# Main stage of a graph layer: a pair's 1/sqrt(variance) from its bits and three Newton steps on VectorE, in place of ScalarE's Ln and Exp and one step

## What is computed

```python
def _layernorm(x, axis=-1, eps=1e-05):
    m = jnp.mean(x, axis=axis, keepdims=True)
    v = jnp.var(x, axis=axis, keepdims=True)
    return (x - m) / jnp.sqrt(v + eps)

# _L0_gnn_ref(feat, dist, W, w_att_src, w_att_dst, src, dst):
ft = (feat @ W).reshape(n, H, OUT)                    # 4 heads of 64
e = e_src[src] + e_dst[dst];  e = where(e >= 0, e, 0.2 * e)
ex = exp(e - emax[dst]);  denom = segment_sum(ex, dst)
out = segment_sum(ft[src] * (ex / denom[dst] * dist), dst)
# _L0_ffn_ref: router (256 -> 128 -> 6), top 2 of 6 experts, three layers of 256 each
x = x + _L0_gnn_ref(_layernorm(x), ...)
x = x + _L0_ffn_ref(_layernorm(x)[None], ...)[0]
```

## Time and profile before

| | us |
|---|---|
| median of three runs | 3443.87 |
| the profiled execution's own time | 3440.41 |
| its span | 3438.6 |
| preparation and features | 0 to about 350 |
| main stage | about 350 to 2623 |
| expert stage | 2623 to 3438.6 |
| busy: PE, DVE, ACT, POOL | 2431.9, 2002.0, 1558.5, 2092.5 |
| L982 gathers, 1568 | 1504.5 |
| L1039 messages, 294 | 672.3 |
| table loads ahead of Ln and Exp, 63 each | 80.8 each |

### The profile page before, as it was taken

How to read it: one execution, slowest core, us unless ns; L and a number is a source line. 1 busy time by engine, 2 the same in 40 slices (tenths; PEclk the granted TensorE clock), 3 DMA queues, 4 the chain that set the end, 5 groups by cost and what they waited for, 6 DMA issues and landing times. The chain is left out here.

```text
span 3438.6 us, 59846 instructions
## 1 busy us (share of the span) xinstructions
PE 2431.9 (71%) x15542; PEld 1943.8 (57%) x15543; DVE 2002.0 (58%) x4402; ACT 1558.5 (45%) x3023; POOL 2092.5 (61%) x2064
## 2 busy tenths in 40 slices
PE   0177466666777777777777777777664999999995
PEld 0155355555555565556555555555553787777774
DVE  0354444555667677777777777777776733333332
ACT  0066223343445455555555555555552554444442
POOL 0000677777777777767666665556530677777775
PEclk9999678778788788878878888887776999999997
DMA  0366455555555555655555554445435044445443
GB/s 27 103 197 214 146 161 159 157 169 164 168 166 179 164 179 173 179 163 168 153 159 151 155 156 142 147 131 152 135 92 86 24 78 79 81 78 81 79 80 48
DMA packets 244778, 457.70 MB, mean 133 GB/s; under 512 B 56010, under 2 KB 161818, under 8 KB 243805
## 3 DMA queue, kind: packets, MB, share of 16 engines
q0 software_dynamic: 114816, 262.31, 31.8%
q1 hardware_dynamic: 89644, 155.19, 14.1%
q10 hardware_dynamic: 40226, 39.16, 3.3%
HBM read 376.24 MB, written 81.66 MB: 133 GB/s over the span
## 5 line engine op out<-in xcount | busy, mean ns | idle before, releaser
L982 POOL DMA_INDIRECT m_rows<-table,src_col x1568 | 1504.5, 960 | 922.8 <-issue 698.0
L1307 PE MATMUL m_A<-m_msg,m_by_edge 128*128 128x260 f32 x3920 | 1240.7, 482 | 297.8 <-DVE m_msg L1039 231.7
L1307 PEld LDWEIGHTS m_A<-m_msg,m_by_edge 128*128 128x128 f32 x3920 | 933.6, 245 | 514.6 <-DVE m_msg L1039 270.9
L1039 DVE TENSOR_TENSOR m_msg<-m_rows,m_A 128x2048 f32<-128x2048 f32 x294 | 672.3, 2287 | 41.5
L1170 ACT ACTIVATE m_apart<-m_drow,nid 128x1024 bf16 x296 | 340.0, 1148 | 420.8 <-SPq L953 420.8
L1294 PE MATMUL m_E<-m_look_parts,m_by_node 128*128 x7080 | 254.3, 167 | 272.2 <-DVE m_by_edge L1009 198.4
L1294 PEld LDWEIGHTS m_E<-m_look_parts,m_by_node 128*128 128x128 bf16 x7080 | 234.5, 97 | 372.0 <-issue 341.3
L1009 DVE TENSOR_TENSOR m_by_edge<-row,m_E 128x512 f32<-128x512 f32 x590 | 401.9, 681 | 5.3 <-ACT m_E L1167 3.2
L1508 POOL DMA_INDIRECT out<-x_con,x_to_i x206 | 329.2, 1598 | 103.4 <-issue 78.8
L1173 ACT ACTIVATE m_by_node<-m_apart,m_one 128x1024 bf16<-128x1024 bf16 x296 | 339.9, 1148 | 9.7
L1178 ACT ACTIVATE m_z<-m_z 128x32 f32<-128x32 f32 x294 | 67.1, 228 | 578.4 <-DVE m_z L1033 482.8
(11 more groups left out here) (243 smaller groups left out, 2357.7 us busy)
## 6 DMA issues: line engine op xcount, KB each, us to landing
m_drow<-edges SPq DMA_DIRECT2D x196, 512.0 KB
m_rows<-table,src_col POOLq DMA_INDIRECT x1568
ydram<-m_y ACTq DMA_DIRECT2D x49, 264.0 KB
m_xb<-xpad ACTq DMA_DIRECT2D x50, 256.0 KB
table<-f_rowbuf SPq DMA_DIRECT2D x14, 910.0 KB, 4.6
xpad<-f_xin SPq DMA_DIRECT2D x14, 896.0 KB, 7.1
out<-m_x ACTq DMA_DIRECT2D x48, 256.0 KB
f_xin<-in_x SPq DMA_DIRECT2D x13, 896.0 KB, 6.0
```

The lines of the kernel that those rows point to most:

```text
L982: nc.gpsimd.indirect_dma_start(rows[:, g % RING, j, :], None, table, bass.IndirectOffsetOnAxis(ap=K.src_col[:, g, j:j + 1], axis=0)).then_ ...
L1039: v.tensor_tensor(msg[q][:, :, 0:D].rearrange("p j (h n) -> p j h n", h=HEADS), rws[:, :, 0:D].rearrange("p j (h n) -> p j h n", h=HEADS), ...
L1307: m = t.matmul(psA[i % 2][:, 0:ROW], by_edge[i % 3][:, j, :], msg[i % 2][:, j, :], start=(j == tiles[0]), stop=(j == tiles[-1]))
```

## The change

ScalarE's `guess` goes from the main stage, with its three semaphores. VectorE computes the first guess of the reciprocal root itself from the bits of the variance (a shift right by one at the end of `take_sums`, a subtraction from the constant 0x5f3759df at the start of `normalize`, both on int32), and does three Newton steps in place of one. The constant `RSQRT_BITS` was in the file already. Nothing else is moved.

```diff
--- before.py
+++ after.py
@@ -904,6 +904,7 @@
         y = sb("y", [P, 2, YW])
         den, stats, mv = sb("den", [P, 2, HEADS]), sb("stats", [P, 2, 6]), sb("mv", [P, 2, 2])
         var, inv, newton = [sb(n, [P, 2]) for n in ("var", "inv", "newton")]
+        half_bits = sb("half_bits", [P, 2], I32)
         yT = sb("yT", [P, 2, 2 * P])
         rhT = sb("rhT", [P, 2 * P])
         plan = sb("plan", [1, PLAN], I32)
@@ -926,7 +927,6 @@
         summed, added = sem("summed"), sem("added")
         drel_made, z_added, z_sloped = sem("drel_made"), sem("z_added"), sem("z_sloped")
         z_kept, wd_made, slot_free = sem("z_kept"), sem("wd_made"), sem("slot_free")
-        asked, given, between = sem("asked"), sem("given"), sem("between")
         plan_in, look_steps = sem("plan_in"), sem("look_steps")
         light_steps, apart_made, node_onehots = sem("light_steps"), sem("apart_made"), sem("node_onehots")
         weights_in, ready = sem("weights_in"), sem("ready")
@@ -1047,7 +1047,7 @@
                 to = flat(sums[:, bass.ds(before % AR, 1), :])
                 v.tensor_tensor(to, to, psA[1 - q][:, 0:ROW], ALU.add).then_inc(added, 1)
 
-            A_STEPS, L_STEPS = 11, 16
+            A_STEPS, L_STEPS = 13, 25
 
             def take_sums(pair, adds):
 
@@ -1076,18 +1076,23 @@
                 for i in range(2):
                     st.did(v.bn_aggr(mv[:, i, :], stats[:, i, :]))
                 st.settle()
-                v.tensor_scalar(var[:, :], mv[:, :, 1], EPS, None, ALU.add).then_inc(asked, 1)
+                st.did(v.tensor_scalar(var[:, :], mv[:, :, 1], EPS, None, ALU.add))
+                st.settle()
+                st.did(v.tensor_scalar(half_bits[:, :], var[:, :].bitcast(I32), 1, None, ALU.arith_shift_right))
                 assert st.n == A_STEPS, st.n
 
             def normalize(pair):
 
                 st = Steps(dve, light_steps, pair * L_STEPS + A_STEPS)
-                dve.wait_ge(given, pair + 1)
-                st.did(v.tensor_tensor(newton[:, :], inv[:, :], inv[:, :], ALU.mult))
-                st.settle()
-                st.did(v.scalar_tensor_tensor(newton[:, :], newton[:, :], -0.5, var[:, :], ALU.mult, ALU.mult))
-                st.settle()
-                st.did(v.scalar_tensor_tensor(inv[:, :], newton[:, :], 1.5, inv[:, :], ALU.add, ALU.mult))
+                st.settle()
+                st.did(v.tensor_scalar(inv[:, :].bitcast(I32), half_bits[:, :], -1.0, RSQRT_BITS, ALU.mult, ALU.add))
+                for _ in range(3):
+                    st.settle()
+                    st.did(v.tensor_tensor(newton[:, :], inv[:, :], inv[:, :], ALU.mult))
+                    st.settle()
+                    st.did(v.scalar_tensor_tensor(newton[:, :], newton[:, :], -0.5, var[:, :], ALU.mult, ALU.mult))
+                    st.settle()
+                    st.did(v.scalar_tensor_tensor(inv[:, :], newton[:, :], 1.5, inv[:, :], ALU.add, ALU.mult))
                 dve.wait_ge(y_stored, 16 * (pair + 1))
                 dve.wait_ge(y_turned, pair + 1)
                 st.settle()
@@ -1207,9 +1212,6 @@
                 relu_router(pair)
                 keep_logits(pair)
 
-            def guess(pair):
-                rsqrt_guess(nc, 2, var, inv, asked, given, between, pair + 1)
-
             count = lambda r: act.snap(r, min_val=0, max_val=NPAIR)
             index = lambda r: act.snap(r, min_val=0, max_val=NPAIR - 1)
 
@@ -1236,8 +1238,6 @@
                         with act.If(count(routed) < count(done)):
                             copy_turned(index(routed))
                     if i % HI == 1:
-                        with act.If(count(done) < count(ready_pairs)):
-                            guess(index(done))
                         with act.If(count(routed) < count(done)):
                             relu_router(index(routed))
                     if i % HI == 2:
@@ -1255,7 +1255,6 @@
                         with act.If(count(routed) < pair):
                             route(index(routed))
                         act.reg_mov(routed, pair)
-                        guess(act.snap(pair, min_val=0, max_val=NPAIR - 1))
                         store_light(act.snap(pair, min_val=0, max_val=NPAIR - 1))
                     act.reg_mov(done, due)
             now = count(done)
```

## The result

| | before | after |
|---|---|---|
| median of the runs, us | 3444.98 (3442.36 to 3450.21) | 3610.64 (3603.95 to 3613.23) |
| ratio to before, 95% interval | | 1.0476 [1.0457, 1.0495] |
| the profiled execution | 3440.41 | 3610.73 |

The change makes the kernel 166 us slower. The forecast was 3418 us, 27 us faster.

A forecast was written before the change was run, and what follows sets the result against it. Gathers were taken to bound the main stage until 1460 us, VectorE after. 35 pairs at 0.64 us (22.4) plus 4.1 for the last pair, 26.5 us, took 3443.9 to 3417.4, written as 3418; range 3405 to 3431.

The forecast's parts named there:

- Bounds of the stages: Main stage: GpSimd's gathers set the time up to 1460 us, VectorE behind it, where its microseconds count.
- The wait that goes: VectorE's L1086 waiting for ScalarE's guess behind 1460 us: 85.6 us, 35 times, 2.45 us each, would be removed.
- The links: Eight added small VectorE instructions per pair, each waiting for the last: 0.20 us for two, 0.195 for six, 1.57 us.
- a sign of being wrong: Among the signs against the forecast: an integer step on VectorE taking over 0.25 us.
- a gather held back by the step: Rival: new tensor_scalars lengthen GpSimd's gathers by 0.2 us each in 13 gather-bound pairs, 5 us, giving 3423; 6%.
- The entrance: VectorE's branch into normalize after L1048: 0.24 us idle, 0.5 at most; gain 0.64 us a pair.
- The last pair: Main stage's end, no items left: 1.77 us instead of 5.87 to the last old step, gain 4.1 us.
- Slower: Rival: VectorE's longer loop body costs code supply, 1.0 us per turn in 26 turns cancelling the gain, 1.5 giving 3456; 5%.
- given back: Rival: TensorE sets the pace after pairs, L1048 waits instead, half of 22.4 us goes, giving 3429; 12%.
- ScalarE's freed time: Rival: it shortens VectorE's L1036 waits for exponentials, 50.5 us, by a quarter, 13 us more, giving 3405; 12%.

The follow-up runs named there:

- e3: Changed kernel with mended waits, step semaphore cleared each pair so waits use constants, VectorE loop body 247 instructions instead of 293: 3402.82 us, ratio 0.9886 to before.
- e17: Changed kernel with mended waits, its 293-instruction loop body shifted by 54 never-run instructions, on a chip like the first: 3394.45 us, ratio 0.9870 to before.
- e2: Changed kernel with only small edits to its waits (mended), VectorE loop body 293 instructions, unshifted: 3587.02 us, ratio 1.0413 to before.
- e15: Changed kernel with mended waits, 293-instruction loop body shifted by 114 never-run instructions, on a slower chip: 4420.91 us, ratio 0.9995 to before.
- e12: Kernel before with mended waits and the step semaphore cleared after each pair, body 223 instructions, repeat of e8: ratio 0.9999 to before.
- e8: Kernel before with mended waits and the step semaphore cleared after each pair, body 223 instructions, on a slower chip: 4375.99 us, ratio 1.0018 to before.
- e5: Changed kernel with mended waits, 293-instruction loop body shifted by 54 never-run instructions, on a slower chip: 4349.54 us, ratio 0.9958 to before.
- e13: Changed kernel with mended waits, 293-instruction loop body unshifted, on a slower chip: 4475.67 us, ratio 1.0119 to before.
- e14: Changed kernel with mended waits, 293-instruction loop body shifted by 54 never-run instructions, on the same chip as e13: 4394.78 us, ratio 0.9937.

## Why the prediction was wrong

**Bounds of the stages: right.** Up to about item 132 the good versions run level with the kernel before (e3 at 1438.7 us, before at 1435.7), and everything is gained behind.

**The wait that goes: right.** L1086's 85.6 us are gone, with all table loads of the main stage.

**The links: right.** 0.20 us from one to the next in the timeline after (1500.14 to 1500.34); the shorter integer steps are 0.16 to 0.20 us. Some of the new L1088 and L1081 take 0.41 and 0.42 instead; their means behind 1460 us are 253 and 280 ns, 0.08 us above the forecast's 0.20 in the worse case. That is over the 0.25 named as a sign of being wrong, and above the upper bound, but it costs little: the same step in e17, which gains, has 289 ns. The long ones stand behind a gather. All 32 steps of L1081 and L1088 over 0.35 us in the kernel after start 0.52 to 0.56 us behind the start of one of GpSimd's gathers and end 0.01 to 0.02 us ahead of its end; so do all 20, 13 and 21 long ones in e17, e3 and e2 (0.52 to 0.53). Seven short ones after start at the same distance, so it isn't enough by itself. The rival had this the other way round, a gather held back by the step.

**The entrance: wrong in size.** I had set 0.24 us behind the *end* of L1048. The first instruction of `normalize` starts 0.33 us behind its *start* (1499.37 to 1499.70), before its 0.42 us are over: it depends on nothing that L1048 writes, and the entrance rows that I used (L1057) wait for just that. That is 0.33 us a pair too much. From L1048's start to y, before has a median of 3.54 us and after 2.38; with 0.20 for the shift the gain is 0.96 us a pair, where I had 0.64. Times 35 it is 33.6 us, with the end 37.7.

**The last pair: right.** L1079 to the last logits took 13.41 us in the earlier trace rows. After:

```profile
2775.50 0.17 DVE L1079 TENSOR_SCALAR m_var<-m_mv 128x2 f32<-128x2 f32 x1
2775.70 0.17 DVE L1081 TENSOR_SCALAR m_half_bits<-m_var 128x2 int32<-128x2 int32 x1
...
2777.87 0.73 DVE L1100 TENSOR_SCALAR m_y<-m_x,m_mv,m_inv 128x256 f32<-128x256 f32 x2
```

```profile
2784.82 0.18 ACT L1208 ACTIVATE lg<-m_L 128x12 f32 x1 [1.21 <-PE m_L L1328]
```

9.32 us, 4.1 less, as forecast.

So the change as such is worth 38 us by its rows, and 39 (e3) to 47 (e17) by the runs; the forecast was 26.5.

**The step that failed** is a cost that the sum put at nothing: VectorE's code supply. It has no term in the 26.5 us and stands only in the rival "Slower", held at 5% because "for it speaks nothing but that such gaps exist". The runs put it at 184 us (e2 less e3), more than four times the gain. The rival named the right row and the right place, and got three things wrong. It took the eight instructions to be a small addition, and did not count the program: 49 more instructions on 251, that take its end from 766 to 815, over a border at 776. It had the price at 1.0 to 1.5 us a turn, as if the cost grew with the code; it is a step, and it was 6.9 us. And it counted the 26 turns behind 1460 us alone: the gathers' slack in front of it covers 16 turns, not 23, because the stalls are larger than that slack. Laid out for the last 25 turns, from item 144 on: 178 us of stalls, less 32 for the change's own gain (33 pairs at 0.96), less 23 by which L1036's wait shrank because VectorE came later, is 123; the two profiled executions differ by 121.9 there. The turns between items 96 and 144 add 57 us of stalls, of which 39 come through, and the first 16 add 7.

The Trainium skill (Runtime: NRT & Kernel Launch, Instruction fetch mechanics) has this rule, and I had not weighed it: the instruction memory is a queue of 32 KiB filled in 16 KiB blocks, and a taken branch whose target is outside the two blocks held stalls until the target is fetched. Body and memory are near enough in its figures (300 instructions are 19 KB) that it deserved its own chance. The trace agrees on the kind of event, at the back edge, once a turn. With blocks of 256 instructions and a border at 520 it would even have given the change's sign, from two blocks touched to three. But it does not agree on the block: a packet is 8.2 KB, and e15 (629 to 922) would lie within the two blocks from 520 to 1032 and be free, while it had 301 packets. What the runs fit is three packets of 128 instructions held for the loop. Five came in each turn where the loop touches four. As an estimate, three held and a fourth brought ahead would be 33 KB and fit both figures; no run tests it.

**Other rivals.** L1048's wait behind 1460 us is 20.9 us (20.2 in the earlier trace rows): nothing was given back there, nor in e3, where it is 15.8. L1036's is 23.1 in the kernel after (50.5 in the earlier trace rows) but 52.4 in e3, so it shrank behind the stalls and not by ScalarE's freed time. A gather takes 963 ns on average, 960 before: it wasn't held back.

## What to carry to other kernels

Before instructions are added to a loop that is written out, count the engine's loop body in the compiled program, every copy and every wait's register instruction, and where it begins and ends against the packet borders. Here 10 instructions of room were left, and passing them turned a gain of 39 us into a loss of 166. An "issue" row on the first instruction behind a back edge, some us long, together with a jump of the instruction queue's packets, is the sign. The cure here was to shorten the body (waits against constants) or to move it. A change should be timed with that done before it is judged slow.

## What the runs showed of the hardware

- VectorE's code comes in packets of 8.2 KB. A loop that touches three is fetched once (58 to 61 packets in the whole run), one that touches four is fetched anew in every turn (299 to 301, 4.9 a turn), whether it has 275 or 300 instructions.
- A refetch stalls twice: 4.2 us (median in the kernel after) ahead of the loop's first VectorE work, L1028, and 2.5 at the border right behind it, together 6.9 us a turn more than before; with 19 instructions in between the second stall is covered (e15).
- A semaphore wait against a value in a register has an instruction of its own ahead; clearing the semaphore and waiting against constants made the body 46 instructions shorter (e2 to e3), and the clearing cost next to nothing (e12 0.9999 [0.9982, 1.0017], e8 1.0018 [1.0003, 1.0032]).
- A small integer tensor_scalar (128x2) takes 0.16 to 0.21 us, and 0.38 to 0.42 us where it starts 0.52 to 0.56 us into a gather and ends with it (all 32 long ones in the kernel after, 7 exceptions).
- Chips differ: the kernel before took 3443 us on some and 4366 to 4423 on others (4369 and 4423 on one and the same), where some of TensorE's instructions come 1.4 to 2.8 us apart (e5). There the same refetches cost less (e13 less e14 81 us; e2 less e17, two sets, 193).
